# Reordering a scan stage's side work and moving two sums of the step size to GpSimd

## The chip, the cores and the metric

One core of a Trainium2 chip runs one program. The metric is the device time of one execution in microseconds (us). Engines are named as the profile names them: PE (TensorE, matrix products; PEld is its weight load), DVE (VectorE), ACT (ScalarE), POOL (GpSimd) and SP (SyncE, here the issuer of most transfers). Each engine runs its own instruction list in order; they wait for each other through semaphores.

## What is computed

Six stages work on x of 16 sequences x 512 tokens x 128 features: two expert feed-forwards around an attention, then two more around a selective scan. The change touches the scan stage only:

```python
x1 = _dwconv_silu(x, conv_w1, conv_b1, 1)
x2 = _dwconv_silu(x, conv_w2, conv_b2, 2)
xc = gate[0] * x1 + gate[1] * x2
...
delta = jax.nn.softplus(dt + b_dt)
...
def step(h, inp):
    dlt_t, B_t, C_t, x_t = inp
    dA = jnp.exp(dlt_t[:, :, None] * A)
    h = h * dA + dlt_t[:, :, None] * B_t[:, None, :] * x_t[:, :, None]
    y_t = jnp.einsum('bdn,bn->bd', h, C_t)
    return (h, y_t)
...
y = y + D_param * xT
y = y * jax.nn.silu(jnp.swapaxes(z, 1, 2))
```

The inner width is 256 (two groups of 128 partitions), there are 16 states, and four taps for each of the two filters. Its output is added to x, which is then normalized and routed to the top 2 of 8 experts for the last feed-forward.

## The kernel before

The scan stage works on one sequence of 512 tokens after another, and within a sequence on one of 16 states (n) after another. `run` writes the order out: for each state every engine does its `main(s, b, n)` and then its `between(s, b, turn, n)`, which holds a slice of side work. Sequences 0 to 2 and 13 to 15 are written out; 3 to 12 are a loop of five turns with two sequences in each. `b` is the half of the double buffers. Side work belongs to other sequences than the one scanned: the filters, projections and step sizes of s + 1, the statistics of s + 2, and the output, the normalization and the router of s - 1.

The state's own chain is as follows. ACT makes the decay dA of the state (`decay`, L1352, two exponentials). DVE makes the two products ux x B (dBx, L1479 and L1482) into PSUM and then the scan over 1024 columns (L1488). POOL multiplies the state with C (HC, L1420). It waits for the scan and also for the dBx of the state after. PE adds HC up in psY (`total`, L1243), two states behind. The buffers of dA, H and HC have four slots. At n = 0 `total` first multiplies xc with the diagonal of D (L1241), after it has waited for y_ready, which `gated` (L1465) sets when it has read psY.

The step size is softplus, written as relu(v) + ln(1 + u) less a correction, with u = exp(-|v|). ACT's `soften` makes |v|, relu(v), u, 1 + u and ln(1 + u), with two table loads. DVE's `step_sizes_1` (L1452) makes the rounding error of 1 + u. `step_sizes_2` makes two sums (L1456, L1457), which give delta and set delta_ready, and then ux = delta x xc (L1459). ACT's first decay of the next sequence waits for delta_ready.

Where the side work stands: PE's filter taps and ACT's emptying of their PSUM go by the tables CONV_STEPS and EMPTY_STEPS (groups 0 to 3 are the filters, 4 and 5 are z). ACT's `silu` stands at state 8 and does filters and z of s + 1, between two table loads. `to_low` is at 11, `soften` at 13. Of the router of s - 1, ACT has act_0 at 6, act_1 at 8 and act_2 (the exponential of the logits, L308) at 10. DVE has dve_2a at 10 (L303, needs PE's logits from pe_1b at 9), dve_2b at 12 (L317 to L330, the top 2; needs act_2) and dve_2c at 14 (L347 to L351). DVE's `mix` (L1446, puts the two filters together) is at 10, `stats` of s + 2 at 6 and its `normalize` at 9. PE's `project` (L1217, needs mix) is at 10 and `steps` (L1223, needs to_low) at 12. SP loads B and C of s + 1 as soon as `to_low` has run, in chunks of two states, and then the rows of s + 3.

Of the kernel before, what the change touches and what calls it, by code (L numbers as in the profile page):

```python
# [792 lines left out]
def attention_stage(nc, k, wqkv, source):  # L793


    with Stage(nc, "att") as st:
# [208 lines left out]
        def _(dve):  # L1005
# [36 lines left out]
            def body(s, b, turn, first, last):  # L1042
# [41 lines left out]
CONV_STEPS = {1: ((0, (0, 1)),), 2: ((0, (2, 3)),), 3: ((1, (0, 1, 2)),), 4: ((1, (3,)), (2, (0, 1))), 5: ((2, (2, 3)), (3, (0,))),  # L1084
              6: ((3, (1, 2, 3)),), 7: ((4, (0,)), (5, (0,)))}
EMPTY_STEPS = {2: (0,), 4: (1,), 5: (2,), 7: (3,), 8: (4, 5)}


def scan_stage(nc, k, w, source):
# [4 lines left out]
    with Stage(nc, "ssm") as st:  # L1094
# [19 lines left out]
        ST, NB = SEQ_TILES, STATES  # L1114
        CHUNK, SLOTS = 2, 4
# [12 lines left out]
        dA_ready, dBx_done, h_ready, hc_ready, y_summed, y_ready, out_summed, added, cleared, z_done = map(  # L1128
            sem, "dA_ready dBx_done h_ready hc_ready y_summed y_ready out_summed added cleared z_done".split())
# [54 lines left out]
        def _(pe):  # L1184
# [49 lines left out]
            def total(s, b, n):  # L1234

                pe.wait_ge(hc_ready, s * NB + n + 1)
                if n == 0:
                    if positive(s):
                        pe.wait_ge(y_ready, s)
                    for dt in range(DT):  # L1240
                        nc.tensor.matmul(psY[:, dt, :], diag[:, dt, :], xc[:, b, dt, :], start=True, stop=False)  # L1241
                for dt in range(DT):
                    last = nc.tensor.matmul(psY[:, dt, :], k.ident[:, :], HC[:, n % RP, (dt + n) % DT, :], start=False, stop=(n == NB - 1))  # L1243
                last.then_inc(y_summed, 1)
# [45 lines left out]
            flip(1)  # L1290
            run(pe, main, between)
# [9 lines left out]
        def _(act):  # L1301
# [12 lines left out]
            def silu(s, b):  # L1314
                act.preload_act_table_set("silu_and_others")
                act.wait_ge(emptied, s * 6 + 6)
                nc.scalar.activation(pre[:, :, :], pre[:, :, :], ACT.Silu).then_inc(silu_done, 1)
                nc.scalar.activation(zs[:, b, :, :], zs[:, b, :, :], ACT.Silu).then_inc(z_done, 1)
                act.preload_act_table_set("natural_log_exp_and_others")
                act.wait_ge(silu_done, s + 1)  # L1320
                nc.scalar.activation(xc[:, b, :, :], pre[:, 0:DT, :], ACT.Identity, scale=gates[:, 0:1]).then_inc(halved, 1)
# [33 lines left out]
            def main(s, b, n):  # L1355
                if n + 1 < NB:
                    decay(s, b, n + 1)
                elif there(s, 1):
                    decay(s + 1, 1 - b, 0)

            def between(s, b, turn, n):
                if there(s, -1):
                    if n == 4:
                        R.norm.act_root(nc, act, s - 1)
                    if n == 6:
                        R.act_0(nc, act, s - 1, 1 - b, turn - 1 + b)
                    if n == 8:
                        R.act_1(nc, act, s - 1, 1 - b)
                    if n == 10:
                        R.act_2(nc, act, s - 1)  # L1370
                if there(s, 1):
                    for g in EMPTY_STEPS.get(n, ()):
                        empty(s + 1, 1 - b, g)
                    if n == 0:
                        to_hT(s + 1)
                    if n == 7 and there(s, 2):
                        N.act_root(nc, act, s + 2)
                    if n == 8:
                        silu(s + 1, 1 - b)
                    if n == 11:  # L1380
                        to_low(s + 1)
                    if n == 13:
                        soften(s + 1)
                if there(s, 2):
                    if n == 11:
                        N.act_apply(nc, act, xn, s + 2).then_inc(normed, 1)
# [9 lines left out]
            for g in range(6):  # L1396
                empty(0, 0, g)
            silu(0, 0)
# [4 lines left out]
            decay(0, 0, 0)  # L1403
            run(act, main, between)
# [7 lines left out]
        def _(pool):  # L1412
# [13 lines left out]
            R.pool_start(pool)  # L1426
            run(pool, main, between)
# [5 lines left out]
        def _(dve):  # L1433
# [15 lines left out]
            def step_sizes_1(s, b):  # L1449

                dve.wait_ge(one_ready, s + 1)
                chain(nc.vector.scalar_tensor_tensor(out=rest[:, :, :], in0=rest[:, :, :], scalar=-1.0, in1=soft, op0=ALU.add, op1=ALU.subtract))  # L1452
# [19 lines left out]
            def main(s, b, n):  # L1472
                if n == 0:
                    dve.wait_ge(ux_ready, s + 1)
                c = n // CHUNK
# [14 lines left out]
            def between(s, b, turn, n):  # L1490
                if there(s, -1):
# [10 lines left out]
                    if n == 12:  # L1502
# [3 lines left out]
                if there(s, 1):  # L1506
                    if n == 10:
                        mix(s + 1, 1 - b)
                    if n == 14:
                        step_sizes_1(s + 1, 1 - b)  # L1510
                    if n == 15:
                        step_sizes_2(s + 1, 1 - b)
                if there(s, 2):
                    if n == 6:
                        stats(s + 2, b, turn + 1)
                    if n == 9:
# [25 lines left out]
            step_sizes_2(0, 0)  # L1542
            stats(1, 1, 0)
            normalize(1)
            links = 4 + 3 + 4 + sum(R.links_0()) + 2
# [99 lines left out]
```

## Time and profile before

| | |
|---|---|
| median of 3 runs | 3467.05 us (3467.03 to 3468.33) |
| the profiled execution | 3465.32 us, its span 3463.5 us |
| mean granted TensorE clock | 0.865 |
| busy: PE, DVE, ACT, POOL | 2444.5, 2279.3, 1532.4, 1684.0 us |

The scan stage lies between about 1750 and 3080 us of the span. The page's slices show it; each digit is the busy share of 1/40 of the span in tenths, PEclk the granted clock of TensorE in tenths:

```profile
PE   2409995666399943199937888777777778738992
DVE  3604445666544468155528999999999999974553
ACT  0005554444255511055535555565555555524551
POOL 1755551333345537455504565655555566654551
PEclk9999997788699965599968889888888889879996
```

A row of a timeline is: start us, duration us, engine, line, operation, out<-in, shape, count of merged instructions, and in brackets the idle time before it with what ended it. "issue" there means that the profile shows nothing that the engine waited for. Where several instructions are merged, as x2 or x4, the duration is of all of them.

### The profile page before, as it was taken

Reading aid. Unit: us, or ns where it says so; the run is one execution under the profiler, and the core shown is the slowest. Engines: PE = TensorE matmul, PEld = TensorE weight load, DVE = VectorE, ACT = ScalarE, POOL = GpSimd, SP = SyncE. Lnnn points to the kernel's source line nnn. Section 1 sums busy time; section 2 is a strip of 40 time slices with the busy share of each in tenths; the row PEclk is TensorE's granted clock in tenths of the full one; section 3 lists DMA queues with packets and bytes.
Section 4 is the critical chain, followed back from the end, with each engine's and each line's share of the span. In section 5 each row is a group of like instructions: output and inputs, shape, how many; then the busy total and the mean of one; then the engine's idle time right before and its main releaser. Section 6 shows DMA issues by size and latency. Waiting matters only on the chain. (4 is left out here: it accounts for less than half of the span.)

```text
span 3463.5 us, 50385 instructions
## 1 busy us (share of the span) xinstructions
PE 2444.5 (71%) x12608; PEld 1746.5 (50%) x12608; DVE 2279.3 (66%) x6241; ACT 1532.4 (44%) x2928; POOL 1684.0 (49%) x1350
## 2 busy tenths in 40 slices
PE   2409995666399943199937888777777778738992
PEld 2309994555389933199913333333333333318992
DVE  3604445666544468155528999999999999974553
ACT  0005554444255511055535555565555555524551
POOL 1755551333345537455504565655555566654551
PEclk9999997788699965599968889888888889879996
DMA  8127871111178732278723333333333333317776
GB/s 260 54 80 230 226 213 51 39 47 37 38 230 227 227 104 78 87 229 227 205 86 105 117 124 124 112 129 110 120 126 122 110 122 116 117 52 217 226 229 178
DMA packets 262510, 478.93 MB, mean 138 GB/s; under 512 B 37309, under 2 KB 173467, under 8 KB 262272
## 3 DMA queue, kind: packets, MB, share of 16 engines
q1 hardware_dynamic: 202576, 388.64, 37.9%
q0 software_dynamic: 34816, 68.00, 5.5%
q10 hardware_dynamic: 25008, 21.11, 1.9%
q8 instruction: 35, 0.57, 0.1%
q14 instruction: 75, 0.61, 0.1%
HBM read 383.22 MB, written 98.54 MB: 139 GB/s over the span
## 5 line engine op out<-in xcount | busy, mean ns | idle before, releaser
L1420 POOL TENSOR_TENSOR ssm_HC<-ssm_H,ssm_BC 128x1024 f32<-128x1024 f32 x256 | 601.4, 2349 | 590.6 <-DVE ssm_psX L1482 541.8
L1243 PE MATMUL ssm_psY<-ssm_HC,ident 128*128 128x512 f32 x1024 | 554.7, 673 | 201.8 <-POOL ssm_HC L1420 201.2
L1488 DVE TENSOR_TENSOR_SCAN ssm_H<-ssm_dA,ssm_psX 128x1024 f32<-128x1024 f32 x256 | 585.3, 2286 | 45.1 <-issue 32.0
L1243 PEld LDWEIGHTS ssm_psY<-ssm_HC,ident 128*128 128x128 f32 x1024 | 205.1, 210 | 499.9 <-POOL ssm_HC L1420 272.4
L1352 ACT ACTIVATE ssm_dA<-ssm_delta,ssm_A 128x511 f32<-128x511 f32 x512 | 329.7, 708 | 102.5 <-DVE ssm_delta L1457 100.0
L374 POOL DMA_INDIRECT xslots<-att_r_xn,att_r_idx x128 | 127.1, 993 | 284.3 <-DVE att_r_idx L351 248.3
L1205 PE MATMUL ssm_psA<-ssm_hT,ssm_Wtap 128*128 128x512 f32 x512 | 245.1, 614 | 2.5 <-ACT ssm_hT L1304 2.5
L709 POOL DMA_INDIRECT d_back<-d_yr,d_to_row x144 | 139.8, 971 | 155.4 <-DVE d_yr L784 131.7
L709 POOL DMA_INDIRECT c_back<-c_yr,c_to_row x144 | 139.8, 971 | 155.1 <-DVE c_yr L784 133.1
L709 POOL DMA_INDIRECT b_back<-b_yr,b_to_row x144 | 139.8, 971 | 154.5 <-DVE b_yr L784 132.6
L709 POOL DMA_INDIRECT a_back<-a_yr,a_to_row x144 | 139.8, 971 | 154.0 <-DVE a_yr L784 132.0
L1479 DVE TENSOR_TENSOR ssm_psX<-ssm_ux,ssm_BC 128x512 f32<-128x512 f32 x256 | 191.4, 748 | 9.3 <-issue 7.7
L753 ACT ACT_TABLE_LOAD x72 | 92.4, 1283 | 223.6 <-PEq L104 222.3
L1310 ACT ACTIVATE ssm_pre<-ssm_psA,ssm_col 128x512 f32<-128x512 f32 x64 | 43.7, 683 | 331.9 <-PE ssm_psA L1205 331.9
L753 ACT ACTIVATE c_H<-c_psH,c_W 128x256 f32<-128x256 f32 x288 | 127.5, 474 | 125.4 <-PE c_psH L730 125.4
L753 ACT ACTIVATE d_H<-d_psH,d_W 128x256 f32<-128x256 f32 x288 | 127.5, 474 | 125.1 <-PE d_psH L730 125.1
L753 ACT ACTIVATE b_H<-b_psH,b_W 128x256 f32<-128x256 f32 x288 | 127.5, 474 | 125.0 <-PE b_psH L730 125.0
L753 ACT ACTIVATE a_H<-a_psH,a_W 128x256 f32<-128x256 f32 x288 | 127.5, 474 | 124.4 <-PE a_psH L730 124.4
L374 POOL DMA_INDIRECT xslots<-to_a_r_xn,to_a_r_idx x128 | 125.2, 978 | 106.7 <-DVE to_a_r_idx L351 65.1
L1482 DVE TENSOR_TENSOR ssm_psX<-ssm_ux,ssm_BC 128x512 f32<-128x512 f32 x256 | 176.6, 690 | 0.0
L1205 PEld LDWEIGHTS ssm_psA<-ssm_hT,ssm_Wtap 128*128 128x128 f32 x512 | 101.8, 201 | 131.5 <-issue 128.2
L374 POOL DMA_INDIRECT xslots<-to_c_r_xn,to_c_r_idx x128 | 126.5, 989 | 83.0 <-issue 41.6
(513 smaller groups left out, 5724.7 us busy)
## 6 DMA issues: line engine op xcount, KB each, us to landing
ssm_BC<-bc_rows SPq DMA_DIRECT2D x128, 1024.0 KB
a_W<-in_l_pack SPq DMA_DIRECT2D x72, 514.0 KB
b_W<-in_l_pack SPq DMA_DIRECT2D x72, 514.0 KB
c_W<-in_l_pack SPq DMA_DIRECT2D x72, 514.0 KB
d_W<-in_l_pack SPq DMA_DIRECT2D x72, 514.0 KB
a_xs<-xslots SPq DMA_DIRECT2D x72, 131.0 KB
b_xs<-xslots SPq DMA_DIRECT2D x72, 131.0 KB
c_xs<-xslots SPq DMA_DIRECT2D x72, 131.0 KB
```

The costliest lines, as they stand in the source:

```text
L374: pool.indirect_dma_start(out=self.k.xslots[:, :], out_offset=bass.IndirectOffsetOnAxis(ap=self.idx[:, b, i:i + 1].bitcast(U32), axis=0), ...
L709: pool.indirect_dma_start(out=target[:, :], out_offset=bass.IndirectOffsetOnAxis(ap=to_row[:, q, s:s + 1].bitcast(U32), axis=0), in_=yr[:, ...
L753: nc.scalar.activation(H[:, b, f, :], psH[:, f, 0:BLOCK], gelu, bias=W[:, q, HIDDEN + FT * D + f:HIDDEN + FT * D + f + 1]).then_inc(h_read ...
L1205: last = nc.tensor.matmul(o, Wtap[:, c, t, dt * P:(dt + 1) * P], hT[:, PAD - back:PAD - back + SEQ], start=(t == 0), stop=(t == TAPS - 1))
L1243: last = nc.tensor.matmul(psY[:, dt, :], k.ident[:, :], HC[:, n % RP, (dt + n) % DT, :], start=False, stop=(n == NB - 1))
L1310: nc.scalar.activation(pre[:, g, :], psA[:, g % 2, :], ACT.Identity, bias=col[:, dt, c:c + 1]).then_inc(emptied, 1)
L1352: last = nc.scalar.activation(dA[:, n % RA, (dt + n) % DT, 1:], delta[:, b, dt, 1:], ACT.Exp, scale=A[:, dt, n:n + 1])
L1420: nc.gpsimd.tensor_tensor(HC[:, n % RP, :, :], H[:, n % RH, :, :], BC[:, n // CHUNK % SLOTS, 1, n % CHUNK:n % CHUNK + 1, :].to_broadcast([ ...
L1479: nc.vector.tensor_tensor(psX[:, 2 * odd, :], ux[:, b, 0, :], BC[:, c % SLOTS, 0, n % CHUNK, :], ALU.mult)
L1482: nc.vector.tensor_tensor(psX[:, 1, :], ux[:, b, 1, :], BC[:, c % SLOTS, 0, n % CHUNK, :], ALU.mult).then_inc(dBx_done, 1)
L1488: nc.vector.tensor_tensor_scan(flat(H[:, n % RH, :, :]), flat(dA[:, n % RA, :, :]), flat(psX[:, odd:odd + DT, :]), 0.0, ALU.mult, ALU.add) ...
```

## The change

It moves side work to other states and two sums to another engine. On ACT the decays are made two states ahead instead of one. The filters end at PE's state 5, z at 6. `silu` stands at state 6 and does the filters of s + 1 and z of s (in two waits), followed by the scaling of xc (now `half`); act_0 is at 7, act_1 at 9, act_2 at 11; `to_low` at 9, `soften` at 10. On DVE `stats` is at 0, `normalize` at 4, `mix` at 8, dve_2b at 11, `step_sizes_1` at 12. On PE `project` is at 8, `steps` at 9, pe_1b at 10, pe_2 at 12, the flip of s + 2 at 13, and the sum of the gathered rows at 15, for s + 3. The diagonal product moves from state 0 to state 9, and the first total of a sequence starts psY. The two sums of the step size leave DVE: POOL makes them after its HC of state 13, and DVE makes ux (`drive`) after dve_2c at state 14.

```diff
-CONV_STEPS = {1: ((0, (0, 1)),), 2: ((0, (2, 3)),), 3: ((1, (0, 1, 2)),), 4: ((1, (3,)), (2, (0, 1))), 5: ((2, (2, 3)), (3, (0,))),
-              6: ((3, (1, 2, 3)),), 7: ((4, (0,)), (5, (0,)))}
-EMPTY_STEPS = {2: (0,), 4: (1,), 5: (2,), 7: (3,), 8: (4, 5)}
+CONV_STEPS = {1: ((0, (0, 1, 2)),), 2: ((0, (3,)), (1, (0, 1))), 3: ((1, (2, 3)), (2, (0,))), 4: ((2, (1, 2, 3)),), 5: ((3, (0, 1, 2, 3)),),
+              6: ((4, (0,)), (5, (0,)))}
+EMPTY_STEPS = {3: (0,), 4: (1,), 5: (2,), 6: (3,), 8: (4, 5)}
...
             def total(s, b, n):
 
                 pe.wait_ge(hc_ready, s * NB + n + 1)
-                if n == 0:
-                    if positive(s):
-                        pe.wait_ge(y_ready, s)
+                if n == 0 and positive(s):
+                    pe.wait_ge(y_ready, s)
+                if n == SKIP:
                     for dt in range(DT):
-                        nc.tensor.matmul(psY[:, dt, :], diag[:, dt, :], xc[:, b, dt, :], start=True, stop=False)
+                        nc.tensor.matmul(psY[:, dt, :], diag[:, dt, :], xc[:, b, dt, :], start=False, stop=False)
...
                     if n == 7:
-                        if there(s, 2):
-                            pe.wait_ge(G.taken, s + 3)
+                        pe.wait_ge(added, s)
                         R.pe_1a(nc, pe, s - 1, 1 - b)
-                    if n == 9:
+                    if n == 10:
                         R.pe_1b(nc, pe, s - 1, 1 - b)
-                    if n == 13:
+                    if n == 12:
                         R.pe_2(nc, pe, s - 1, 1 - b)
...
-                    if n == 10:
+                    if n == 8:
                         project(s + 1, 1 - b)
-                    if n == 12:
+                    if n == 9:
                         steps(s + 1)
                 if there(s, 2):
-                    if n == 4:
+                    if n == 13:
+                        flip(s + 2)
+                if there(s, 3):
+                    if n == 15:
                         if there(s, -1):
-                            pe.wait_ge(added, s)
-                        G.pe(nc, pe, s + 2, b, turn + 1, psR4)
-                    if n == 15:
-                        flip(s + 2)
+                            pe.wait_ge(R.rowed, s)
+                        G.pe(nc, pe, s + 3, 1 - b, turn + 1 + b, psR4)
...
             def silu(s, b):
+
                 act.preload_act_table_set("silu_and_others")
+                if there(s, 1):
+                    act.wait_ge(emptied, s * 6 + 10)
+                    nc.scalar.activation(pre[:, :, :], pre[:, :, :], ACT.Silu).then_inc(silu_done, 1)
                 act.wait_ge(emptied, s * 6 + 6)
-                nc.scalar.activation(pre[:, :, :], pre[:, :, :], ACT.Silu).then_inc(silu_done, 1)
                 nc.scalar.activation(zs[:, b, :, :], zs[:, b, :, :], ACT.Silu).then_inc(z_done, 1)
                 act.preload_act_table_set("natural_log_exp_and_others")
+                if there(s, 1):
+                    half(s + 1, 1 - b)
...
             def main(s, b, n):
-                if n + 1 < NB:
-                    decay(s, b, n + 1)
+
+                if n + 2 < NB:
+                    decay(s, b, n + 2)
                 elif there(s, 1):
-                    decay(s + 1, 1 - b, 0)
+                    decay(s + 1, 1 - b, n + 2 - NB)
...
+                    if n == 9:
+                        to_low(s + 1)
+                if there(s, -1):
+                    if n == 4:
+                        R.norm.act_root(nc, act, s - 1)
+                    if n == 7:
+                        R.act_0(nc, act, s - 1, 1 - b, turn - 1 + b)
+                    if n == 9:
+                        R.act_1(nc, act, s - 1, 1 - b)
+                    if n == 11:
+                        R.act_2(nc, act, s - 1)
+                if n == 6:
+                    silu(s, b)
+                if there(s, 1) and n == 10:
+                    soften(s + 1)
...
+                if n == 13 and there(s, 1):
+                    step_sizes_2(s + 1, 1 - b)
+
+            def step_sizes_2(s, b):
+                pool.wait_ge(l_ready, s + 1)
+                pool.wait_ge(rest_ready, s + 1)
+                nc.gpsimd.tensor_tensor(rest[:, :, :], absv, rest[:, :, :], ALU.subtract).then_inc(less_ready, 1)
+                pool.wait_ge(less_ready, s + 1)
+                nc.gpsimd.tensor_tensor(delta[:, b, :, :], rest[:, :, :], v[:, :, :], ALU.add).then_inc(delta_ready, 1)
...
-            def step_sizes_2(s, b):
-                dve.wait_ge(l_ready, s + 1)
-                chain(nc.vector.tensor_tensor(rest[:, :, :], absv, rest[:, :, :], ALU.subtract))
-                nc.vector.tensor_tensor(delta[:, b, :, :], rest[:, :, :], v[:, :, :], ALU.add).then_inc(delta_ready, 1)
+                nc.vector.scalar_tensor_tensor(out=rest[:, :, :], in0=rest[:, :, :], scalar=-1.0, in1=soft, op0=ALU.add, op1=ALU.subtract).then_inc(rest_ready, 1)
+
+            def drive(s, b):
                 dve.wait_ge(delta_ready, s + 1)
                 nc.vector.tensor_tensor(ux[:, b, :, :], delta[:, b, :, :], xc[:, b, :, :], ALU.mult).then_inc(ux_ready, 1)
...
-                    if n == 12:
+                    if n == 11:
                         R.dve_2b(nc, dve, chain, s - 1, 1 - b)
                     if n == 14:
                         R.dve_2c(nc, dve, chain, s - 1, 1 - b)
                 if there(s, 1):
-                    if n == 10:
+                    if n == 8:
                         mix(s + 1, 1 - b)
+                    if n == 12:
+                        step_sizes_1(s + 1, 1 - b)
                     if n == 14:
-                        step_sizes_1(s + 1, 1 - b)
-                    if n == 15:
-                        step_sizes_2(s + 1, 1 - b)
+                        drive(s + 1, 1 - b)
                 if there(s, 2):
-                    if n == 6:
+                    if n == 0:
                         stats(s + 2, b, turn + 1)
-                    if n == 9:
+                    if n == 4:
                         normalize(s + 2)
```

## Rows read from the trace of the kernel before

**Rows 1.** Busy time by stretch: us, busy by engine, granted clock, DMA share, GB/s.

```profile
1818.00:3072.00 1254.00, 965.45 (x2482) 422.32 (x2482) 1173.24 (x1725) 695.14 (x1104) 726.37 (x367) 0.87 0.35 116
2609.10:2688.10 79.00, 62.10 (x162) 27.17 (x162) 74.60 (x113) 45.22 (x73) 46.71 (x24) 0.88 0.37 121
2661.50:2665.00 3.50, 3.50 (x5) 1.28 (x6) 3.46 (x4) 0.09 (x1) 2.34 (x1) 0.50 0.00 0
```

**Rows 2.** Timeline of DVE, line L1459 (ux), for sequences 0, 1, 14 and 15.

```profile
1809.91 1.22 DVE L1459 TENSOR_TENSOR ssm_ux<-ssm_delta,ssm_xc 128x1024 f32<-128x1024 f32 x1
1889.68 1.23 DVE L1459 TENSOR_TENSOR ssm_ux<-ssm_delta,ssm_xc 128x1024 f32<-128x1024 f32 x1
...
2926.09 1.22 DVE L1459 TENSOR_TENSOR ssm_ux<-ssm_delta,ssm_xc 128x1024 f32<-128x1024 f32 x1
3002.74 1.22 DVE L1459 TENSOR_TENSOR ssm_ux<-ssm_delta,ssm_xc 128x1024 f32<-128x1024 f32 x1
```

**Rows 3.** Timeline of DVE, the sequence from 2609.1 us.

```profile
2616.85 1.23 DVE L1465 TENSOR_TENSOR ssm_v<-ssm_psY,ssm_zs 128x1024 f32<-128x1024 f32 x1 [0.29 <-PE ssm_psY L1243]
2617.99 0.69 DVE L1479 TENSOR_TENSOR ssm_psX<-ssm_ux,ssm_BC 128x512 f32<-128x512 f32 x1
...
2621.60 0.75 DVE L1479 TENSOR_TENSOR ssm_psX<-ssm_ux,ssm_BC 128x512 f32<-128x512 f32 x1
...
2640.00 0.66 DVE L483 TENSOR_TENSOR X<-X,ssm_psR 128x512 f32 x1
...
2642.80 0.69 DVE L1479 TENSOR_TENSOR ssm_psX<-ssm_ux,ssm_BC 128x512 f32<-128x512 f32 x1
...
2649.95 0.99 DVE L1479 TENSOR_TENSOR ssm_psX<-ssm_ux,ssm_BC 128x512 f32<-128x512 f32 x1
...
2657.51 2.29 DVE L1488 TENSOR_TENSOR_SCAN ssm_H<-ssm_dA,ssm_psX 128x1024 f32<-128x1024 f32 x1 [1.47 <-issue]
...
2666.12 2.29 DVE L1488 TENSOR_TENSOR_SCAN ssm_H<-ssm_dA,ssm_psX 128x1024 f32<-128x1024 f32 x1
...
2671.46 0.69 DVE L1479 TENSOR_TENSOR ssm_psX<-ssm_ux,ssm_BC 128x512 f32<-128x512 f32 x1
...
2684.28 1.26 DVE L1456 TENSOR_TENSOR ssm_rest<-ssm_pre,ssm_rest 128x1024 f32<-128x1024 f32 x1
2685.58 1.23 DVE L1457 TENSOR_TENSOR ssm_delta<-ssm_rest,ssm_v 128x1024 f32<-128x1024 f32 x1
...
2689.92 0.70 DVE L1479 TENSOR_TENSOR ssm_psX<-ssm_ux,ssm_BC 128x512 f32<-128x512 f32 x1 [1.86 <-issue]
```

**Rows 4.** Timeline of ACT, the same sequence.

```profile
2639.59 0.69 ACT L1310 ACTIVATE ssm_pre<-ssm_psA,ssm_col 128x512 f32<-128x512 f32 x1 [4.96 <-PE ssm_psA L1205]
...
2641.40 1.64 ACT L182 ACTIVATE ssm_r_xn<-X,ssm_r_shift,ssm_r_rstd 128x128 f32 x4
...
2644.48 1.32 ACT L1352 ACTIVATE ssm_dA<-ssm_delta,ssm_A 128x511 f32<-128x511 f32 x2
...
2649.58 1.28 ACT L1315 ACT_TABLE_LOAD   x1
...
2656.10 2.54 ACT L1352 ACTIVATE ssm_dA<-ssm_delta,ssm_A 128x511 f32<-128x511 f32 x4
...
2670.61 1.27 ACT L1333 ACTIVATE ssm_pre<-ssm_psA,ssm_col 128x512 f32<-128x512 f32 x2 [0.77 <-PE ssm_psA L1223]
...
2678.74 1.33 ACT L1352 ACTIVATE ssm_dA<-ssm_delta,ssm_A 128x511 f32<-128x511 f32 x2
```

**Rows 5.** Timeline of POOL, the same sequence.

```profile
2676.42 2.35 POOL L1420 TENSOR_TENSOR ssm_HC<-ssm_H,ssm_BC 128x1024 f32<-128x1024 f32 x1 [1.24 <-DVE ssm_psX L1482]
```

**Rows 6.** Timeline of PE, the same sequence.

```profile
2625.66 1.88 PE L1243 MATMUL ssm_psY<-ssm_HC,ident 128*128 128x512 f32 x4
2627.37 2.74 PE L1205 MATMUL ssm_psA<-ssm_hT,ssm_Wtap 128*128 128x512 f32 x6
...
2661.44 3.70 PE L1217 MATMUL ssm_psA<-ssm_xc,ssm_Wx 128*96 128x512 f32 x4 [5.20 <-DVE ssm_xc L1446]
```

More of the change, by code:

```diff
@@ L1114, in scan_stage @@
         ST, NB = SEQ_TILES, STATES
+        SKIP = 9
         CHUNK, SLOTS = 2, 4
@@ L1236, in total @@
                 pe.wait_ge(hc_ready, s * NB + n + 1)
-                if n == 0:
-                    if positive(s):
-                        pe.wait_ge(y_ready, s)
+                if n == 0 and positive(s):
+                    pe.wait_ge(y_ready, s)
+                if n == SKIP:
                     for dt in range(DT):
-                        nc.tensor.matmul(psY[:, dt, :], diag[:, dt, :], xc[:, b, dt, :], start=True, stop=False)
+                        nc.tensor.matmul(psY[:, dt, :], diag[:, dt, :], xc[:, b, dt, :], start=False, stop=False)
                 for dt in range(DT):
-                    last = nc.tensor.matmul(psY[:, dt, :], k.ident[:, :], HC[:, n % RP, (dt + n) % DT, :], start=False, stop=(n == NB - 1))
+                    last = nc.tensor.matmul(psY[:, dt, :], k.ident[:, :], HC[:, n % RP, (dt + n) % DT, :], start=(n == 0), stop=(n == NB - 1))
                 last.then_inc(y_summed, 1)
@@ L1290, in _ @@
             flip(1)
+            G.pe(nc, pe, 2, 0, 1, psR4)
             run(pe, main, between)
@@ L1375, in between @@
                         to_hT(s + 1)
-                    if n == 7 and there(s, 2):
-                        N.act_root(nc, act, s + 2)
[L1378 to L1385, printed above, removed]
+                    if n == 9:
[13 more added lines that the diff above has]
+                    soften(s + 1)
+                if there(s, 2):
+                    if n == 2:
+                        N.act_root(nc, act, s + 2)
+                    if n == 5:
                         N.act_apply(nc, act, xn, s + 2).then_inc(normed, 1)
@@ L1395, in _ @@
             to_hT(0)
-            for g in range(6):
+            for g in range(4):
                 empty(0, 0, g)
-            silu(0, 0)
+            act.preload_act_table_set("silu_and_others")
+            act.wait_ge(emptied, 4)
+            nc.scalar.activation(pre[:, :, :], pre[:, :, :], ACT.Silu).then_inc(silu_done, 1)
+            act.preload_act_table_set("natural_log_exp_and_others")
+            half(0, 0)
+            for g in range(4, 6):
+                empty(0, 0, g)
             to_low(0)
@@ L1403, in _ @@
             decay(0, 0, 0)
+            decay(0, 0, 1)
             run(act, main, between)
@@ L1451, in step_sizes_1 @@
                 dve.wait_ge(one_ready, s + 1)
-                chain(nc.vector.scalar_tensor_tensor(out=rest[:, :, :], in0=rest[:, :, :], scalar=-1.0, in1=soft, op0=ALU.add, op1=ALU.subtract))
-            def step_sizes_2(s, b):
-                dve.wait_ge(l_ready, s + 1)
-                chain(nc.vector.tensor_tensor(rest[:, :, :], absv, rest[:, :, :], ALU.subtract))
-                nc.vector.tensor_tensor(delta[:, b, :, :], rest[:, :, :], v[:, :, :], ALU.add).then_inc(delta_ready, 1)
+                nc.vector.scalar_tensor_tensor(out=rest[:, :, :], in0=rest[:, :, :], scalar=-1.0, in1=soft, op0=ALU.add, op1=ALU.subtract).then_inc(rest_ready, 1)
+            def drive(s, b):
                 dve.wait_ge(delta_ready, s + 1)
@@ L1472, in main @@
             def main(s, b, n):
+                c = n // CHUNK
                 if n == 0:
                     dve.wait_ge(ux_ready, s + 1)
-                c = n // CHUNK
                 if n % CHUNK == 0:
@@ L1541, in _ @@
             step_sizes_1(0, 0)
-            step_sizes_2(0, 0)
+            drive(0, 0)
             stats(1, 1, 0)
             normalize(1)
-            links = 4 + 3 + 4 + sum(R.links_0()) + 2
+            links = 2 + 3 + 4 + sum(R.links_0()) + 2
             run(dve, main, between, chain, 2 * links)
```

15 lines of the change are left out of this document (4 added, 11 removed).

## The prediction

> **What bounds the kernel now.** I read the busy table by stretches first. Over the scan stage VectorE (DVE) is busy 1173.24 of 1254.00 us, TensorE (PE) 965.45, GpSimd (POOL) 726.37, ScalarE (ACT) 695.14; in one sequence VectorE has 74.60 of 79.00 us [rows 1]. So only this stage, only VectorE's order, and what it waits for can move the time. Next I read VectorE's timeline: the product L1459 opens each sequence; from the one before sequence 1 to the one before sequence 14 it is 1036.4 us (1889.68 to 2926.09), sequence 0 takes 79.8 and sequence 14 takes 76.65 [rows 2]. There are four sequences that begin at the loop's back edge with a gap of 1.86 us put down to issue, after a wait-free product [rows 3]. Last, inside the sequence from 2609.1: a wait of 0.29 us for y and one of 1.47 us before state 10's scan, and no other above 0.2 us [rows 3]. The 1.47 us wait is at a scan whose decay ScalarE has not made: the decay follows a ScalarE block of table loads and silu from 2649.58 to 2656.10 [rows 4].
>
> **Without the waits, the new VectorE order.** A state costs 3.6 us (2617.99 to 2621.60) [rows 3]. The sequence of 79.0 us, less 1.47, less 0.29, less the two sums of 1.26 and 1.23 that leave (with their gaps 2.55), is 74.7 us. If nothing new waited, that were 4.3 us less for each sequence. Two new waits speak against it, and both come out of the order of instructions.
>
> **Wait one, at GpSimd's sums.** VectorE's two sums L1456 and L1457 go; GpSimd makes them after its product HC(13). HC(13) starts only when the second dBx of state 14 is done; one such product took 2.35 us [rows 5]. A subtract and an add of the same 128x1024 f32 form are not in the trace on GpSimd. Their bounds: 1.23 us each (VectorE's own, [rows 3]) and 3.6 us (one product of 2.35 plus a held stretch the size of VectorE's sum). I take 2.35, the row of the same engine and size. From the start of state 14 on VectorE: dBx 1.35, HC 2.35, subtract 2.35, add 2.35, three handovers of about 0.15 (an estimate from the tenths of a microsecond between dependent rows): 8.8 us to delta. VectorE itself is there after the scan (3.6) and the position sums of the router (five instructions of at most 128x64, about 0.2 us each: 1.0, an estimate): at 4.6. It waits **4.2 us** where it used to work 2.5 us on the sums. Behind that wait stand ux, state 15 and the next sequence; ScalarE waits in decay 0 of the next sequence, which now stands in state 14, and GpSimd's HC(14) waits for VectorE's state 15. ScalarE then has 1.2 us of work per decay and VectorE 4.8 us before it needs the first, so the decays cause no third wait. So the order in which the work moves to the engine that is half as fast, by itself, pays 4.2 to save 2.55.
> The Trainium skill (GPSIMD Engine Reference, "Elementwise — side-by-side cycle accounting") says a two-input add of 2048 f32 takes GpSimd 4497 ns and VectorE 2293; half of it is an estimate of 2.25 us and 1.15 us for this size. The trace has 2.35 and 1.23 [rows 3, 5], so it nearly agrees. By the page's figure the wait would be 4.0 us, and the total 3 us less. It speaks against moving such sums at all.
>
> **Wait two, at the router's exponentials.** The new ScalarE order puts soften(s+1) into state 10 and R.act_2(s-1), which the router's top-k needs, into state 11; R.dve_2b, which waits for it, goes from state 12 to state 11 on VectorE. Before, act_2 stood at state 10 and soften at 13. So top-k now waits for the whole softplus of the next sequence. When is that? I count from the start of the sequence on VectorE, t = 0.
> Step a: state 0 (3.6), stats of s+2, which now stand at state 0 (2.8: 2640.00 to 2642.80), state 1 (3.6), gated (1.2): y_ready at **11.2** [rows 3]. TensorE's total(0) now starts with a write of psY and waits for y_ready.
> Step b: TensorE then has, without a gap, total 0 to 3, out, and 13 taps of the filter (one of filter 0, four each of 1, 2, 3). A matmul of 512 columns takes 0.43 us (4 of them in 1.71 us, 2625.66 to 2627.37) [rows 6]; total and out are 4 such each, a tap 2: 20 + 26 = 46, times 0.43 = 19.8. Filter 3 is done at **31.0**. HC(3) is ready at 24.6, so it doesn't hold this up.
> Step c: ScalarE, in its order: empty group 3 with decay 9, 1.81; table, silu, silu of z, table, half, 6.52; act_0, 3.08; decay 10, 1.22; empty groups 4 and 5, two of 0.6 less their overlap, 1.1: 13.7, so emptied at **44.7** [rows 4]. VectorE's mix at state 8 is done at 42.7 and doesn't set it.
> Step d: TensorE: project 1.75, total(7) 1.72, steps 1.75: 5.2, at full clock **50.0** with the handovers. The project row took 3.70 us after 5.20 us of idling, and the granted clock there is 0.50, the lower level of 1.2 GHz [rows 1, 6]. In the new order TensorE idles some 5 us before pe_1a, then works 2 us, then waits again, so I add 1: **51.0**. Ends: 0 and 5.2.
> Step e: ScalarE: soften from abs to the last table load 8.13 (2670.61 to 2678.74), decay 13 1.22, and for act_2 (a 32-column exponential, an estimate from the shorter rows) and the handovers 0.4 [rows 4]: **60.8**.
> VectorE would be there at 12 states of 3.6, plus stats 2.8, gated 1.14, add and statistics 2.66, normalize 1.0, dve_0 1.4, mix and 2a 1.5: 53.7. So **7 us** of waiting, part of it already in 2a, since pe_1b stands behind steps on TensorE.
> Step f, from there to the next sequence: 2b 3.1 (scan at 2666.12 plus 2.2, to 2671.46), state 12 3.6, step_sizes_1 1.25, state 13 3.6, to delta 8.8, ux 1.25, state 15 3.6: 25.2 [rows 3]. Period **86.0 us**.
>
> **The rest costs nothing or little.** Decays two ahead: the 1.47 us wait ends, since decay 10 is made at 43.6 and needed at 47.5. Stats at state 0, normalize at 4: same VectorE work; the sum of the rows on TensorE moves to state 15, where that engine idles (5.20 us idle even at its busy part, [rows 6]). The wait of 0.29 us for y goes, behind the stats. The matmuls with diag move from state 0 to 9: same number, 1.7 us, at TensorE between totals that are there early; without that cover they would come on step d. Silu of z in its own sequence: same instructions. SP's queue keeps its order; load of s+3 waits for taken, which comes earlier. Before the loop: silu needn't wait for z, -3, sums on GpSimd, +2: -1.
>
> **The sum.** Sequences 1 to 13: 13 x 86.0 = 1118.0, plus 4 back edges of 1.9 = 1125.6, against 1036.4: +89.2. Sequence 14 has no stats: 83.2 against 76.65: +6.6. Sequence 0 has no router: its own waits before (79.8 in all, [rows 2]) against 65 of work plus 5 at delta, and 5.4 more for its start and ScalarE: about 75.4, -4.4. Sequence 15, no s+1: -0.5. Prologue -1. Together +90. The profiled run is 3465.3 us (span 3463.5), so 3555; the median of the runs is 1.7 above it: **3557 us**.
>
> **Rivals.**
> (1) *Softplus is no obstacle; only the GpSimd wait is left.* If TensorE and ScalarE ran the chain some 7 us ahead of my count, the period were 53.9 + 25.2 = 79.1: 13 x 79.1 + 7.6 - 1036.4 = 0; with the ends -6: **3460**, about no change, and faster if GpSimd's sums take 1.23 us too (2.24 less in each of 15 sequences, 3426). It decides at exped before 53.9. For it: ScalarE is busy only 45.22 us of 79 [rows 1]. Against: those are in one order and none of a to e overlaps. 0.08, half of that under 3460.
> (2) *Part of the chain is shorter*, because out or the taps fit in front of y_ready, or empties before act_0 are early: 2.5 to 5 us off: 3492 to 3525. 0.15.
> (3) *More than counted:* TensorE at 0.50 for all of step d: +4.2 more a sequence, 3612; or VectorE's small instructions between the sums are held. For the second: the dBx row beside a product took 0.99 instead of 0.70 us (2649.95 against 2689.92, [rows 3]). If the position sums had to wait for both GpSimd sums, +0.6 a sequence: 3565. The Trainium skill (GPSIMD Engine Reference, "Specifications") says that GpSimd shares its interfaces with VectorE instructions of two SBUF inputs; that is this mechanism, and the trace agrees with it in this one size. 0.15 for both.
> (4) *The order does not do what it says:* the sums move, but GpSimd is late for HC and VectorE waits there. HC's ring is four deep and GpSimd has 32 us free in 79 [rows 1]; 0.02.
>
> **How the numbers follow.** My forecast, 3557 (its own range 3535 to 3585), has 0.6. The range to hold 8 in 10 takes in most of (2) and (3): 3510 to 3595. A measurement of this kernel can tell about 0.2% from no change, 7 us. Faster: 0.06, from (1); same: 0.04; slower: 0.90.
>
> **What would show it.** Right: VectorE's timeline has a gap of some 4 us before each ux (L1459's line) put down to GpSimd's delta, and one or two gaps of together 7 us at the router's top L303 and pv L317 in states 10 and 11, put down to TensorE's logits and ScalarE's prob; the scan's 1.4 us wait is gone; a period of 86 us in the loop. Wrong: ScalarE's act_2 lies within 54 us of the sequence's start (then rival 1), or the subtract and the add on GpSimd are far from 2.35 us, or y_ready isn't what total(0) waited for.

## The result

The changed kernel took 3570.59 us (median of 4 runs, 3568.72 to 3572.12), the kernel before 3467.69 us on the same chip: ratio 1.0296, 95% interval 1.0278 to 1.0314. It is slower by 103 us. Forecast were 3557 us and a range of 3510 to 3595.

The profile after, first the busy time by stretch (us, then PE, PEld, DVE, ACT and POOL busy, granted clock, DMA share, GB/s), which answers to [rows 1]. The second stretch is one sequence from state 0 to state 0; the third is TensorE after its pause for y_ready:

```profile
1818.00:3160.00 1342.00, 985.86 (x2458) 430.63 (x2459) 1175.04 (x1676) 708.34 (x1115) 793.83 (x393) 0.87 0.32 109
2678.05:2764.80 86.75, 62.02 (x162) 27.81 (x162) 75.89 (x112) 45.61 (x72) 51.87 (x27) 0.90 0.33 110
2689.30:2694.60 5.30, 5.29 (x21) 3.79 (x22) 5.14 (x6) 0.11 (x1) 3.86 (x3) 0.68 0.15 41
```

A sequence takes 86.75 us, where it took 79.0. GpSimd is busy 51.87 us instead of 46.71, mostly for the two sums (2.35 and 2.34 us). VectorE shows 75.89 us of work instead of 74.60, although 2.5 us of sums have left it. That is where a reader must not stop: part of this "work" is waiting, as the timeline shows.

The waits of VectorE in the stage, from 1814.5 us on (engine, line, waited for: us in total, times, longest):

```profile
DVE ssm_r_top L303 <- PE ssm_psR L279: 78.3, 14, 6.5
DVE ssm_r_pv L317 <- ACT ssm_r_prob L308: 41.6, 14, 3.0
DVE ssm_ux L1483 <- POOL ssm_delta L1450: 10.9, 2, 6.0
DVE ssm_psX L1503 <- issue: 3.6, 4, 1.0
DVE ssm_H L1512 <- issue: 2.1, 1, 2.1
```

The two waits at the router are there, in each of sequences 1 to 14: 5.6 us for the logits (L303) and 3.0 us for the exponentials (L317). Sequence 15 has router work too, but no step sizes of a next sequence stand ahead of it, and it waits at neither line. The scans now wait only twice, both in sequence 0: 1.8 us for a decay, and 2.1 us that the list puts down to issue. In the kernel before they waited 32.0 us in 17 times, and 1.8 us for that same first decay.

What stands ahead of the router shows on TensorE and on ScalarE. TensorE makes the step sizes (L1224) and a total before the logits (L279); ScalarE runs the whole softplus (L1342 to the table load L1353) and a decay before the exponentials (L308):

```profile
2728.56 1.98 PE L1224 MATMUL ssm_psA<-ssm_low,ssm_Wdt 64*128 64x512 f32 x4
2732.29 0.95 PE L279 MATMUL ssm_psR<-gate_w,ssm_r_xnT 128*128 128x8 f32 x8
...
2730.58 1.26 ACT L1342 ACTIVATE ssm_pre<-ssm_psA,ssm_col 128x512 f32<-128x512 f32 x2 [1.07 <-PE ssm_psA L1224]
...
2737.42 1.28 ACT L1353 ACT_TABLE_LOAD   x1
2738.72 1.33 ACT L1361 ACTIVATE ssm_dA<-ssm_delta,ssm_A 128x511 f32<-128x511 f32 x2
2739.95 0.21 ACT L308 ACTIVATE ssm_r_prob<-ssm_r_L 128x32 f32<-128x32 f32 x1
```

The wait before ux, which I had forecast for all sequences, shows in two places only, in the prologue (5.99 us) and at the end of sequence 0 (4.90 us), where no router work stands ahead of it. In the others VectorE's timeline at the end of state 14 reads so:

```profile
2752.97 2.29 DVE L1512 TENSOR_TENSOR_SCAN ssm_H<-ssm_dA,ssm_psX 128x1024 f32<-128x1024 f32 x1
2755.18 0.20 DVE L347 TENSOR_TENSOR ssm_r_pos<-ssm_psR,ssm_r_run 128x64 f32<-128x64 f32 x1
2755.41 0.17 DVE L348 TENSOR_TENSOR ssm_r_run<-ssm_psR,ssm_r_run 128x16 f32<-128x16 f32 x1
2755.50 2.24 DVE L349 TENSOR_TENSOR ssm_r_pos<-ssm_r_pos,ssm_r_hot 128x64 f32<-128x64 f32 x1
2757.78 0.22 DVE L350 TENSOR_REDUCE ssm_r_row<-ssm_r_pos 128x8 f32<-128x64 f32 x1
2758.03 2.07 DVE L351 CAST ssm_r_idx<-ssm_r_row 128x8 int32<-128x8 f32 x1
2760.11 1.22 DVE L1483 TENSOR_TENSOR ssm_ux<-ssm_delta,ssm_xc 128x1024 f32<-128x1024 f32 x1
```

and GpSimd's in the same microseconds:

```profile
2753.02 2.34 POOL L1437 TENSOR_TENSOR ssm_HC<-ssm_H,ssm_BC 128x1024 f32<-128x1024 f32 x1 [1.24 <-DVE ssm_psX L1506]
2755.32 2.35 POOL L1448 TENSOR_TENSOR ssm_rest<-ssm_pre,ssm_rest 128x1024 f32<-128x1024 f32 x1
2757.74 2.34 POOL L1450 TENSOR_TENSOR ssm_delta<-ssm_rest,ssm_v 128x1024 f32<-128x1024 f32 x1
```

L349, a product of 128x64, takes 2.24 us and ends 0.07 us after GpSimd's subtract does; L351, a cast of 128x8, takes 2.07 us and ends with GpSimd's add. Without GpSimd's sums both take 0.2 us (e2_sums_on_vector). The 4.0 us of waiting for delta are all there (2756.1 to 2760.11), but the profile counts them as busy.

### The profile page after: what moved, and what is told of

Read it like the earlier page. It is cut to its first block and busy times, and to the rows that moved or that the text cites. A ratio compares the mean times of both kernels' runs of the same rounds, so it can differ in the third digit from the quotient of the medians.

```text
span 3568.9 us, 50404 instructions
## 1 busy us (share of the span) xinstructions
PE 2475.7 (69%) x12608; PEld 1757.6 (49%) x12608; DVE 2290.8 (64%) x6209; ACT 1541.0 (43%) x2930; POOL 1764.9 (49%) x1382
## 5 line engine op out<-in xcount | busy, mean ns | idle before, releaser
L1244 PE MATMUL ssm_psY<-ssm_HC,ident 128*128 128x512 f32 x1024 | 582.0, 699 | 199.3 <-POOL ssm_HC L1437 160.5
L1206 PE MATMUL ssm_psA<-ssm_hT,ssm_Wtap 128*128 128x512 f32 x512 | 236.7, 601 | 0.7 <-ACT ssm_hT L1306 0.7
L1506 DVE TENSOR_TENSOR ssm_psX<-ssm_ux,ssm_BC 128x512 f32<-128x512 f32 x256 | 176.2, 688 | 0.0
L374 POOL DMA_INDIRECT xslots<-ssm_r_xn,ssm_r_idx x128 | 151.1, 1180 | 35.4 <-issue 22.4
```

The lines of the kernel that those rows point to most:

```text
L374: pool.indirect_dma_start(out=self.k.xslots[:, :], out_offset=bass.IndirectOffsetOnAxis(ap=self.idx[:, b, i:i + 1].bitcast(U32), axis=0), ...
L1206: last = nc.tensor.matmul(o, Wtap[:, c, t, dt * P:(dt + 1) * P], hT[:, PAD - back:PAD - back + SEQ], start=(t == 0), stop=(t == TAPS - 1))
L1506: nc.vector.tensor_tensor(psX[:, 1, :], ux[:, b, 1, :], BC[:, c % SLOTS, 0, n % CHUNK, :], ALU.mult).then_inc(dBx_done, 1)
```

## The experiments

Each edit is a short diff against the changed kernel unless it says otherwise. The chips differ in how long the rest of the program takes (the kernel before took 3603.9, 3576.8, 3471.6 and 3600.8 us on them), so each run is compared with the kernel before on its own chip. The difference lies outside the scan stage: e1_router_first and e8_pool_sums_early both take what the kernel before takes on their chips, their spans differ by 133 us, and of these 118 lie ahead of the first ux (1934.8 against 1816.8 us) and 17 behind the last. Below, "the stretch" is the time from the ux before sequence 1 to the ux before sequence 14. It is 1036.4 us in the kernel before and 1131.2 in the changed kernel (1131.1 on a second chip), and it can be compared across chips to about 3 us: e3_both has 1016.0 us on one and 1019.1 on another.

**The router ahead of softplus** (e1_router_first):

```diff
-                    if n == 10:
+                    if n == 9:
                         R.pe_1b(nc, pe, s - 1, 1 - b)
...
-                    if n == 11:
+                    if n == 10:
                         R.act_2(nc, act, s - 1)
```

> The changed kernel (3570.6 us) with two steps of the router of s - 1 pulled ahead of the softplus of s + 1: ScalarE's act_2 from state 11 to state 10, before soften, and TensorE's pe_1b from state 10 to state 9, before steps. GpSimd keeps the two sums. Theory (the new order costs 8.6 us a sequence in the waits at L303 and L317, because softplus stands ahead of the router): a rest of 1.8 us at L303 stays, since pe_1b is done at about 55 us of the sequence; the period falls from 86.7 to about 79.9, 14 times 6.8 is 95 us less: 3475 us, range 3450 to 3490. Rival (the slowdown is GpSimd's sums and its contention with VectorE, and the waits at the router only take up what is lost elsewhere): no more than 20 us less, 3550 or above.

Measured: 3603.63 against 3603.9 us, ratio 0.9999 (0.9988 to 1.001). The stretch takes 1037.6 us, 79.8 a sequence, where the changed kernel takes 1131.2. The wait at L317 is gone, at L303 19.2 us in 12 waits remain. Two lines that change the order of two engines take back the whole slowdown. The rival falls: GpSimd's sums are still in this kernel.

**The sums back on VectorE** (e2_sums_on_vector). The two sums leave GpSimd's list, and `drive` on VectorE makes them:

```diff
             def drive(s, b):
-                dve.wait_ge(delta_ready, s + 1)
+                dve.wait_ge(l_ready, s + 1)
+                dve.wait_ge(rest_ready, s + 1)
+                nc.vector.tensor_tensor(rest[:, :, :], absv, rest[:, :, :], ALU.subtract).then_inc(less_ready, 1)
+                dve.wait_ge(less_ready, s + 1)
+                nc.vector.tensor_tensor(delta[:, b, :, :], rest[:, :, :], v[:, :, :], ALU.add).then_inc(delta_ready, 1)
+                dve.wait_ge(delta_ready, s + 1)
```

> The changed kernel with its new order, but the two sums back on VectorE, before ux in state 14. Theory: the sums on GpSimd cost 4.1 us of waiting (spread over L349 and L351, which show 2.24 and 2.07 us) to save 2.5 us of work: 1.6 less in each of 15 sequences, 3546 us, range 3538 to 3556, and L349 and L351 take about 0.2 us each again. The waits at L303 and L317 stay at 8.6 us. Rival (GpSimd's sums are the slowdown): back to 3470 to 3490 us. A third reading, that L349 and L351 are long for another reason than GpSimd's sums, would leave them above 2 us.

Measured: ratio 1.0204 (1.0187 to 1.0221), 77 us over the kernel before; expected were 78. The stretch takes 1106.2 us, 1.9 less a sequence than in the changed kernel. The two router lines are short again:

```profile
L349 DVE TENSOR_TENSOR ssm_r_pos<-ssm_r_pos,ssm_r_hot x16: 215/216/217, 2094.6 to 3295.5; 128x64 f32<-128x64 f32 x16
L351 DVE CAST ssm_r_idx<-ssm_r_row x16: 171/172/172, 2095.1 to 3296.0; 128x8 int32<-128x8 f32 x16
```

against the changed kernel (durations in ns are least/median/most):

```profile
L349 DVE TENSOR_TENSOR ssm_r_pos<-ssm_r_pos,ssm_r_hot x16: 215/2243/2296, 1972.6 to 3201.2; 128x64 f32<-128x64 f32 x16
L351 DVE CAST ssm_r_idx<-ssm_r_row x16: 170/2074/2076, 1975.2 to 3201.7; 128x8 int32<-128x8 f32 x16
```

**Both** (e3_both, and e3_again on another chip):

> Both edits at once: the router ahead of softplus and the two sums on VectorE. Theory, with the costs independent: 3475 less 24, 3451 us, range 3425 to 3465, so 0.5% faster than the kernel before (3467.7), because the scan's wait for a decay (1.4 to 2.3 us a sequence) and the wait for y stay away. Rival (the two costs overlap): the sum of the two single gains isn't reached, 3480 us or more.

> The kernel e3_both, unedited, on the chip of the next two, so that the three can be compared. Theory: 0.992 to 0.994 of the kernel before.

Measured: 0.9924 (0.9907 to 0.994) and 0.9916 (0.9901 to 0.9932), 28 us under the kernel before each time, 1016.0 and 1019.1 us for the stretch. The gains of e1 and e2 add up: against the changed kernel's stretch e1 saves 93.6 us, e2 25.0, together 118.6, and both edits at once 115.2 and 112.1. So the two costs are independent to within some 6 us of 119. This version is faster than both kernels.

**ScalarE's half alone** (e4_act2_first_only): only act_2 moves from 11 to 10; pe_1b stays at 10.

> The changed kernel with only ScalarE's act_2 moved from state 11 to state 10, before soften; TensorE's pe_1b stays at state 10, behind steps. GpSimd keeps the sums. Theory (two separate obstacles in series: TensorE's steps before pe_1b, ScalarE's soften before act_2): the wait at L303 stays at 5.6 us, the wait at L317 (3.0 us) goes, 14 times 3.0 is 42 us less: 3529 us, range 3515 to 3540. If soften, now behind act_2, were late for decay 13, a scan wait would take its place and the time stay at 3550 to 3575.

Measured: ratio 1.0149 (1.0132 to 1.0166). L317's wait is gone, L303's stays (71.7 us in 14 waits). The stretch is 1085.9 us, 3.5 less a sequence, where I had expected 3.0; L303's waits are shorter too, by 6.6 us in all. So the obstacles stand in series, as said: TensorE's step-size product ahead of the logits, then softplus ahead of the exponentials. No scan waited in exchange.

**GpSimd's sums alone, in the old order** (e5_before_pool_sums): the kernel before, with the two sums behind HC of state 14 on GpSimd.

> The kernel before, in its own order, with only the two sums moved to GpSimd, behind its product of state 14; VectorE makes ux in state 15 as before. This is the second half of the change alone. Theory: product, subtract and add on GpSimd (3 x 2.35 with handovers, from the second dBx of state 15) end 7.3 us after that dBx, VectorE used to be done with its two sums 4.8 us after it: 2.4 us more in each of 15 sequences, +36 us, 3504 us, range 3490 to 3515. Rival (a sum taken off the busiest engine is a gain): 2.5 less for each, 3430 us.

Measured: 3608.76 against 3576.84 us, ratio 1.0088 (1.0068 to 1.0107), +32 us. Here nothing stands between the scan and ux on VectorE, so the wait shows openly:

```profile
2727.77 2.29 DVE L1495 TENSOR_TENSOR_SCAN ssm_H<-ssm_dA,ssm_psX 128x1024 f32<-128x1024 f32 x1
2734.90 1.23 DVE L1466 TENSOR_TENSOR ssm_ux<-ssm_delta,ssm_xc 128x1024 f32<-128x1024 f32 x1 [4.85 <-POOL ssm_delta L1433]
```

4.85 us idle in place of 2.5 us of sums.

**GpSimd's sums one state earlier** (e8_pool_sums_early), against e1_router_first:

```diff
-                if n == 13 and there(s, 1):
+                if n == 12 and there(s, 1):
                     step_sizes_2(s + 1, 1 - b)
```

> The kernel e1_router_first with GpSimd's two sums one state earlier, behind its product of state 12, so that delta is there before VectorE asks for it. Theory (GpSimd's two-input sums hold VectorE's two-input products for as long as they run, as L349's 2.24 us suggest): the dBx products of state 14, L1503 and L1506, take 2 to 3 us each instead of 0.7, the wait before ux goes, and the time stays within 12 us of e1_router_first, ratio 0.997 to 1.003. Rival (no contention, GpSimd's sums are hidden by the move): 4 us less in each of 15 sequences, ratio 0.983.

Measured: ratio 1.0000 (0.9991 to 1.001), as e1_router_first (0.9999). Behind the prologue VectorE no longer has to wait for delta, and gains nothing:

```profile
2764.03 0.74 DVE L1503 TENSOR_TENSOR ssm_psX<-ssm_ux,ssm_BC 128x512 f32<-128x512 f32 x1
2764.68 2.83 DVE L1506 TENSOR_TENSOR ssm_psX<-ssm_ux,ssm_BC 128x512 f32<-128x512 f32 x1
2767.55 2.29 DVE L1512 TENSOR_TENSOR_SCAN ssm_H<-ssm_dA,ssm_psX 128x1024 f32<-128x1024 f32 x1
...
2770.07 2.02 DVE L349 TENSOR_TENSOR ssm_r_pos<-ssm_r_pos,ssm_r_hot 128x64 f32<-128x64 f32 x1
```

One half of state 14's dBx is held from 2764.68 to 2767.51, while GpSimd subtracts:

```profile
2764.17 2.79 POOL L1448 TENSOR_TENSOR ssm_rest<-ssm_pre,ssm_rest 128x1024 f32<-128x1024 f32 x1
2767.04 2.67 POOL L1450 TENSOR_TENSOR ssm_delta<-ssm_rest,ssm_v 128x1024 f32<-128x1024 f32 x1
2769.67 2.34 POOL L1437 TENSOR_TENSOR ssm_HC<-ssm_H,ssm_BC 128x1024 f32<-128x1024 f32 x1
```

I had expected both halves at 2 to 3 us; only the second was, since the first began before the subtract. The scan ran beside the add unharmed at 2.29 us, and the product HC(13), pushed behind the sums, then held L349 for 1.8 us. GpSimd's own two sums took 2.79 and 2.67 us here, instead of 2.34. So in these runs GpSimd's 4.7 us were free only beside scans, and HC already takes up that place.

**TensorE kept at work in its pause** (e7_warm_pe): three spare products of 512 columns before it waits for y_ready.

> The changed kernel with three spare products of 512 columns on TensorE in the pause before it waits for y_ready (2.6 us of work into psR, which out overwrites; they compute nothing that is used). In the changed kernel total(0) and out take 2.73 and 2.87 us instead of 1.88 and 1.95 after that pause, and filter 3 is done 33 us after the sequence's start, not 31. Theory (the late filter is due to the lower granted clock after the pause, and what hangs on filter 3 sets the wait at L317): 1.5 to 1.9 us less in each of 14 sequences, 20 to 27 us under the changed kernel on the same chip. Rival (the chain to L317 isn't set by TensorE's filters): the same time as the changed kernel within 6 us. If the spare work holds up total(0) instead, some us more.

> The changed kernel once more, unedited, as the base for the other three on this chip. Theory: 2.8 to 3.1% over the kernel before, 103 us more.

Measured: 1.0298 (1.0282 to 1.0313) against 1.0285 (1.027 to 1.0301) for the changed kernel on the same chip (99 us over the kernel before, where I had expected 103): no gain, so the expectation on the time failed. What the spare work was to show is in the trace all the same. TensorE of the changed kernel, then of e7:

```profile
2689.31 2.73 PE L1244 MATMUL ssm_psY<-ssm_HC,ident 128*128 128x512 f32 x4 [2.88 <-DVE ssm_v L1489]
2691.83 2.87 PE L1231 MATMUL ssm_psR<-ssm_Wout,ssm_v 128*128 128x128 f32 x16
```

```profile
2685.31 1.96 PE L1244 MATMUL ssm_psY<-ssm_HC,ident 128*128 128x512 f32 x4 [0.29 <-DVE ssm_v L1494]
2687.10 1.95 PE L1231 MATMUL ssm_psR<-ssm_Wout,ssm_v 128*128 128x128 f32 x16
...
2716.50 3.62 PE L1244 MATMUL ssm_psY<-ssm_HC,ident 128*128 128x512 f32 x4
...
2764.60 3.69 PE L1244 MATMUL ssm_psY<-ssm_HC,ident 128*128 128x512 f32 x4 [1.80 <-POOL ssm_HC L1442]
```

In the changed kernel the granted clock was 0.68 over these two (the third stretch of the table above), in e7 it was 1.00. Filter 3 is then emptied 31.3 us after the sequence's start instead of 33.0, and that sequence takes 85.8 us instead of 86.7. But total(6) after the later pause now takes 3.62 us instead of 3.04, and in the next sequence the slow stretch lies on total(15), which delays y_ready itself; that sequence takes 88.3 us. The lower clock has moved, it has not gone.

The changed kernel's own loop shows the same two kinds of sequence in turn. In the one after the sequence above the pause for y_ready is as long, 2.87 us, and yet nothing behind it is slow; the slow stretch comes later, at total(6), with a granted clock of 0.50 (2809.0 to 2812.8 us), and filter 3 is emptied 31.3 us after the start:

```profile
2777.09 1.96 PE L1244 MATMUL ssm_psY<-ssm_HC,ident 128*128 128x512 f32 x4 [2.87 <-DVE ssm_v L1489]
2778.88 1.95 PE L1231 MATMUL ssm_psR<-ssm_Wout,ssm_v 128*128 128x128 f32 x16
...
2808.28 3.62 PE L1244 MATMUL ssm_psY<-ssm_HC,ident 128*128 128x512 f32 x4
```

So the pause alone doesn't decide it. Why the sequences alternate, these runs don't tell.

**Two attempts to better e3_both.** e6_act0_early moves act_0 from 7 to 5 on ScalarE; e10_router_in_gap also moves act_1 from 9 to 8 and pe_1b from 9 to 8.

> The kernel e3_both (router ahead of softplus, sums on VectorE) with ScalarE's act_0 moved from state 7 to state 5, ahead of silu. Theory: TensorE's pe_1a and so its later products come earlier, z is emptied about 2 us earlier and project starts earlier by as much; the rest at L303 (17.8 us in 13 waits) goes; mix may wait 0.6 us for the scaled xc. 5 to 12 us under e3_both: 0.989 to 0.992 of the kernel before, where e3_both had 0.9924. Rival (the later silu block delays mix, and with it all that hangs on project, by as much as act_0 takes): 3 us more a sequence, 0.997 to 1.005.

> The kernel e6_act0_early with two more steps of the router pulled ahead: ScalarE's act_1 from state 9 to 8, before z is emptied, and TensorE's pe_1b from 9 to 8, before project, where TensorE idles 5.0 us. In e6_act0_early that idle time stood right before project, which then took 3.4 to 3.7 us instead of 1.9. Theory: the rest of 19.7 us in 14 waits at L303 goes, since the logits no longer stand behind project; 10 to 20 us under e6_act0_early (0.9951): 0.989 to 0.992, and a little under e3_both. Rival (project stays the late one and step sizes or the scan wait for it instead): 0.994 to 0.997.

Measured: e6 0.9951 (0.9937 to 0.9965) and 1027.3 us for the stretch, so worse than e3_both's 1016.0 and 1019.1, against my theory and short of the full rival. mix waits 13.3 us in 15, and project, which now follows an idle time of 5.03 us, takes 3.4 to 3.7 us:

```profile
2649.38 3.73 PE L1218 MATMUL ssm_psA<-ssm_xc,ssm_Wx 128*96 128x512 f32 x4 [5.03 <-ACT ssm_zs L1314]
```

e10 0.9922 (0.9908 to 0.9935): the waits at L303 are gone, but mix waits 18.4 us in 15 instead, and the scans 6.8 us in 12 more than in e3_both. It equals e3 on the same chip (0.9916), within the intervals. It lies between the theory (0.989 to 0.992) and its rival (0.994 to 0.997).

**One part of the new order in the kernel before** (e11_before_decays_two_ahead), a diff against the kernel before:

```diff
-                if n + 1 < NB:
-                    decay(s, b, n + 1)
+                if n + 2 < NB:
+                    decay(s, b, n + 2)
                 elif there(s, 1):
-                    decay(s + 1, 1 - b, 0)
+                    decay(s + 1, 1 - b, n + 2 - NB)
...
             decay(0, 0, 0)
+            decay(0, 0, 1)
```

> The kernel before with one part of the change alone: ScalarE makes the decays two states ahead instead of one. Theory: the scan of state 10 no longer waits for its decay (32.0 us in 17 waits in the kernel before), nothing else changes: 0.991 to 0.994 of the kernel before. Rival (the wait was covered or moves to the scan of state 11): 0.998 to 1.001.

Measured: 0.9922 (0.9905 to 0.9938), 1013.8 us for the stretch. The scan's waits for a decay are gone but for the first one of the stage; VectorE's longest waits behind it are these:

```profile
DVE ssm_psX L1480 <- issue: 7.9, 4, 2.1
DVE ssm_v L1466 <- PE ssm_psY L1243: 4.5, 14, 0.4
DVE ssm_n_stats L147 <- DVE X L483: 2.3, 15, 0.2
```

Three changed lines and one new one give what the best version of the whole new order gives (0.9924 and 0.9916). The rest of the order adds nothing that these runs could tell; with the sums on VectorE it cost 77 us over the kernel before until the router was pulled ahead (e2_sums_on_vector). Its other parts were not tried one by one, so a gain of one and a loss of another may hide in it.

## Why the prediction was right, and where it was off

**The bound** was right: the time went with VectorE's waits. From the changed kernel to e1_router_first, for example, the waits at L303 and L317 fall by 100.7 us in all, and the time from the ux before sequence 1 to the one before sequence 15 by 100.4.

**Wait one** was right in size: from the start of state 14 to ux it took 8.5 us (2751.60 to 2760.11), forecast 8.8. GpSimd's sums took 2.35 and 2.34 us, the value taken from [rows 5]. The form was not: it shows as two stretched instructions, not as an idle time. The rival that both sums hold VectorE's small instructions was therefore right as a mechanism. Its price of 0.6 us was not paid: the subtract held L349, the add held the cast, each ended as GpSimd's sum did, and ux could start with delta. Neither held row stood behind both sums. e5 and e8 show the two faces of the cost, openly waiting or held.

**Wait two** was right in cause, shown by e1 and e4, and nearly in size: 8.6 us against 7. Step by step in the sequence from 2678.05: y_ready at 11.1 (forecast 11.2); filter 3 at 33.0 (31.0); emptied at 46.7 (44.7); soften starts at 52.5 (51.0); L317 at 62.2 (60.8). The term of the sum that was mis-sized here is step b, by 2.0 us: I counted all of it at full clock, but total(0) and out ran at the lower one after the pause of 2.88 us for y_ready. e7 bears this out: with the clock kept, filter 3 came at 31.3. The 1 us that I added for the clock stood in step d, where project and steps of this sequence ran at full speed, and took back part of the miss. In the next sequence, from 2765.88, it is the other way round: step b was right (filter 3 at 31.3), and step d, with total(6) at 3.62 us and project at 2.65, took 7.1 us where I had 6.3; soften started at 52.1, and L317 was at 61.8. From 2243.88 us to the end of the loop the sequences alternate between the two. So the lower clock cost more than the 1 us that I had given it in both kinds, but not in one step.

**The sum.** Sequences 1 to 13: forecast 1125.6, measured 1131.2, so +94.8 (forecast +89.2). Sequence 14: +6.2 (forecast +6.6). Sequence 0 needs a care that I did not take: the new order has ux ahead of state 15 and no longer behind it, so from ux to ux sequence 0 is one state (3.6 us) short, 76.25 us against 79.77, and what follows the last ux is one state long. With this put right sequence 0 was to give back 4.4 us and gave nothing (+0.1): besides the wait for delta (4.90) it had one-off waits of 1.8, 2.1, 1.4 and 1.0 us. Sequence 15 and what follows it took 0.3 less (forecast 0.5 less). The first ux stands 4.6 us later. Of these 2.0 us lie ahead of the stage's own chain (the first normalized rows are transposed at 1768.21 and not at 1766.23). The other 2.6 us are the prologue, where I said 1 less. About 1.3 of them are its first filter, for which ScalarE waited 6.54 us instead of 5.19; that wait is 5.2 to 6.5 us in the other runs, in either order, so it need not be the change's. These sum to 105.4, the difference of the spans, 3568.9 and 3463.5. The forecast of 90 for it was thus near in part by luck: the back edges came out 4 us cheaper than I had counted, which took back some of what the loop's sequences and the prologue cost more.

**A term with the wrong reason.** I counted the back edge's gap as 1.9 us as before; it is 0.9 (3.6 us in four).

**Rival 1** (only the GpSimd wait is left, about no change) is what e1 then made true by hand: 79.8 a sequence with the back edges, where 79.1 and 7.6 us of back edges make 79.7, and a ratio of 0.9999. Rival 2 fell. Rival 3 was right in its first half only in that there was more slow clock than I had counted: in step d, of which it spoke, 0.8 us more in every other sequence and not 4.2 in each. Rival 4 fell: VectorE has no wait for HC.

## What to carry to other kernels

When side work is reordered, follow each engine's list in order and ask for every wait what now stands in front of what it waits for: a 0.2 us exponential behind an 8.1 us softplus cost 3 us, and the logits behind another sequence's product 5.6. Before elementwise work moves from a full VectorE to a GpSimd with time to spare (busy 46.71 of 79.0 us before), ask whether it is off the chain and what of VectorE's work it runs beside; here it was on the chain or held VectorE, and cost 26 to 32 us. And try the parts of a reordering alone: here one part of four lines gave as much as the whole.

## What the runs showed of the hardware that was not expected

- A GpSimd instruction with two SBUF inputs holds a VectorE instruction that starts beside it until its own end: L349 takes 2.24 instead of 0.22 us and ends 0.07 us after the subtract, L1506 takes 2.83 instead of 0.69. It held the cast of 128x8, which has one input, too: 2.07 instead of 0.17. It didn't hold the scans (2.29 us in all runs, one input of theirs in PSUM), L347 and L348 (one input in PSUM), nor the reduction L350. The profile books the time as VectorE's work. The row of 0.99 us in [rows 3] is the same thing, small: the GpSimd product beside it ended at 2650.37 us and the row at 2650.94. The Trainium skill (GPSIMD Engine Reference, "Specifications") names contention with VectorE instructions of two SBUF inputs or in a 2-port mode. The trace agrees for L349 and L1506, with these sizes; in which mode the cast ran, no run here shows.
- The gap at the loop's back edge depends on what VectorE does last. From the start of its last instruction to the first of the next turn it is 3.1 to 3.2 us behind ux (1.22 us long) in the kernel before and 3.1 to 3.3 behind a scan (2.29 us long) in the changed one, so a longer last instruction leaves a smaller gap. That is not a constant: in e8_pool_sums_early it is 3.5 to 3.9 us behind the same scan, and no run shows why.
- TensorE's granted clock fell to 0.50 or partly so behind pauses of 2.9 to 5.1 us, but not behind each: the same product behind the same pause (2.88 and 2.87 us) took 2.73 us in one sequence and 1.96 in the next. Filling one pause moved the low stretch to another place.
